# Joint pass with a ring of forty gathered rows, W1 loaded behind the routing loop, and a reordered combining stage

## The reference, cut to what matters

```python
xn = layernorm(x)
x = x + gat(xn, edges, W1, att_src1, att_dst1, b1, W2, att_src2, att_dst2, b2) \
      + mix(xn, w_qkv, w_proj, b_proj, proj_mat)
x = x + moe(layernorm(x), Wr, br, W1, b1, W2, b2, ln_g, ln_b)

def gat(x, edges, ...):       # two layers; self loops are added
    h = elu(gat_layer(x, ..., 4 heads of 512, concatenated))
    return gat_layer(h, ..., 1 head of 768)
def gat_layer(x, src, dst, W, a_src, a_dst, bias):
    h = x @ W
    e = leaky_relu((h * a_src).sum(-1)[src] + (h * a_dst).sum(-1)[dst], 0.2)
    ex = exp(e - segment_max(e, dst)[dst])
    alpha = ex / (segment_sum(ex, dst)[dst] + 1e-16)
    return segment_sum(h[src] * alpha, dst) + bias
def mix(x, ...):              # linear attention, 12 heads of 64, 256 random features
    q, k, v = x @ w_qkv.T
    q1, k1 = features(q), features(k)      # exp(dash - diag - max) + 1e-4
    return (q1 @ (k1.T @ v) / (q1 @ k1.sum(0))) @ w_proj.T + b_proj
def moe(x, ...):              # 8 experts, 768 -> 192 -> 768, the best two of each token
    out = sum over the two of weight * (gelu(x @ W1[e] + b1[e]) @ W2[e] + b2[e])
    return layernorm(out) * ln_g + ln_b
```

## Time and profile before

| | us |
|---|---|
| median of 3 runs (lowest, highest) | 4027.84 (4027.04, 4029.59) |
| the profiled execution, its time | 4029.73 |
| the profiled execution, its span in the trace | 4027.9 |
| TensorE busy in the span | 3300.9 (82%) |
| VectorE busy | 1924.8 (48%) |
| GpSimd busy | 1510.0 (37%) |
| ScalarE busy | 1126.3 (28%) |

### The profile page before, as it was taken

The page is one execution under the profiler, slowest core; times in us unless marked ns, Lnnn a source line. Parts: engine busy times, 40 slices in busy tenths (PEclk is TensorE's granted clock), DMA queues, the critical chain, the costliest instruction groups (busy, mean ns, idle before and its releaser), DMA issues. The chain is left out here.

```text
span 4027.9 us, 62736 instructions
## 1 busy us (share of the span) xinstructions
PE 3300.9 (82%) x21812; PEld 2631.4 (65%) x21813; DVE 1924.8 (48%) x4387; ACT 1126.3 (28%) x2419; POOL 1510.0 (37%) x1514
## 2 busy tenths in 40 slices
PE   7966889889889879999799967887888878569940
PEld 7964666666666658899799955555555545459940
DVE  4844555555555554444322214444444444543347
ACT  2332333333333333333322212222222221313321
POOL 1334656565556400000000025555555552223346
PEclk9988999999999989999899977888898889569975
DMA  6656776776777465444666647777777774837667
GB/s 196 217 174 194 217 224 210 219 224 208 217 225 216 146 185 151 131 133 123 181 99 86 87 135 227 240 246 233 240 238 248 233 235 133 271 112 242 239 220 256
DMA packets 276409, 786.75 MB, mean 195 GB/s; under 512 B 81807, under 2 KB 94818, under 8 KB 272903
## 3 DMA queue, kind: packets, MB, share of 16 engines
q0 software_dynamic: 97216, 416.71, 33.9%
q1 hardware_dynamic: 178886, 366.15, 30.8%
HBM read 676.48 MB, written 167.42 MB: 210 GB/s over the span
## 5 line engine op out<-in xcount | busy, mean ns | idle before, releaser
L937 POOL DMA_INDIRECT k_rows<-tab,k_pick x576 | 583.8, 1014 | 429.3 <-PE k_num L1392 231.3
L2182 POOL DMA_INDIRECT m_rows<-tab,a_e x500 | 498.4, 997 | 449.9 <-PE m_out L2501 249.8
L1392 PE MATMUL k_num<-k_rows,k_wt 128*32 128x385 f32 (+1 forms) x3200 | 346.9, 496 | 71.3 <-issue 51.3
L1392 PEld LDWEIGHTS k_num<-k_rows,k_wt 128*32 128x32 f32 x3200 | 109.7, 110 | 243.0 <-issue 209.1
L142 PE MATMUL g_prod<-g_w_hi,g_h_h 128*128 128x384 f32 x768 | 258.7, 337 | 11.0 <-DVE g_h_l L1802 11.0
L143 PE MATMUL g_prod<-g_w_lo,g_h_h 128*128 128x384 f32 x768 | 258.2, 336 | 0.0
L144 PE MATMUL g_prod<-g_w_hi,g_h_l 128*128 128x384 f32 x768 | 258.1, 336 | 0.0
L1654 PE MATMUL f_prod<-f_a_h,f_w_hi 128*128 128x512 f32 (+1 forms) x672 | 253.8, 378 | 1.8 <-DVE f_w_lo L1597 1.7
L1655 PE MATMUL f_prod<-f_a_l,f_w_hi 128*128 128x512 f32 (+1 forms) x672 | 246.4, 367 | 0.0
L1656 PE MATMUL f_prod<-f_a_h,f_w_lo 128*128 128x512 f32 (+1 forms) x672 | 246.4, 367 | 0.0
L2481 PE MATMUL m_pj<-a_w,m_at 128*128 128x384 f32 x600 | 220.1, 520 | 18.1 <-DVE m_x L2292 17.8
(11 more groups left out here) (367 smaller groups left out, 7596.2 us busy)
## 6 DMA issues: line engine op xcount, KB each, us to landing
agg<-k_outb SPq DMA_DIRECT2D x100, 384.0 KB
f_a_in<-agg SPq DMA_DIRECT2D x100, 384.0 KB, 7.3
g_h<-h SPq DMA_DIRECT2D x25, 1024.0 KB, 12.2
ys<-e_y SPq DMA_DIRECT2D x56, 384.0 KB
h<-f_e SPq DMA_DIRECT2D x16, 1024.0 KB, 5.2
tab<-q_xn SPq DMA_DIRECT2D x25, 388.5 KB, 5.8
tab<-g_row SPq DMA_DIRECT2D x25, 385.5 KB, 4.5
m_own<-tab SPq DMA_DIRECT2D x25, 385.5 KB, 7.4
```

The lines of the kernel that those rows point to most:

```text
L937: pool.indirect_dma_start(rows[:, place(u, n), :], None, dram["tab1"], at, bounds_check=bound, oob_is_err=False).then_inc(rows_in[i], 16)
L1392: mm = pe.matmul(num[i][o, 0:n], wt[u % 2][:, v, o], rows[:, place(u, 2 * (half + v) + g), a:a + n], start=(v == 0), stop=(v == 1), tile_p ...
L2182: pool.indirect_dma_start(rows[:, place(h, c) + k, :], None, tab, bass.IndirectOffsetOnAxis(ap=e[h % 4][:, 0, k * SLOTS + c:k * SLOTS + c ...
```

## The change

In the joint pass the ring has 40 places. Room for it comes from x in three buffers instead of four, and from single buffers for `qt_h`, `att` and `own`; of `own` the two last columns, which the logits need, have a small double buffer of their own (`own_al`). The waits follow: `qt_high` for the products that read `qt_h`, `divide` for the turns that read `att`, `load_own` for the sums of the tile before. GpSimd adds the bias to x behind the gathers of a stage instead of before them. In SP's order `own` is last and the store stands before x. In the routing stage the six loads of W1 stand behind the loop. Six tiles of x for the combining stage are loaded at the end of the experts' stage, into buffers of a pool around both; the combining stage has six buffers for x and three for y, and VectorE adds the second expert of tile t+1 before it finishes tile t.

```diff
@@ mix_out
-    RING = 36
-    XR = 4
+    RING = 40
+    XR = 3
-        qt_h = s.sb2("qt_h", [P, KC, P], F32R)
+        qt_h = s.sb("qt_h", [P, KC, P], F32R)
-        att, at = s.sb2("att", [P, D]), s.sb("at", [P, KC, P])
+        att, at = s.sb("att", [P, D]), s.sb("at", [P, KC, P])
-            ald, own = s.sb2("ald", [P, P]), s.sb2("own", [P, TROW2])
+            ald, own, own_al = s.sb2("ald", [P, P]), s.sb("own", [P, D + 1]), s.sb2("own_al", [P, 2])
@@ mix_out, sync
-                def load_own(h):
+                def load_ends(h):
                     if h >= 2:
                         sp.wait_ge(acc_done, 2 * (h - 1))
                     sp.dma_start(ald[h % 2][:, :], ...).then_inc(ald_in[h % 2], 16)
-                    sp.dma_start(own[h % 2][:, :], tab[h * P:(h + 1) * P, :]).then_inc(own_in[h % 2], 16)
+                    sp.dma_start(own_al[h % 2][:, :], tab[h * P:(h + 1) * P, D + 1:D + 3]).then_inc(own_al_in[h % 2], 16)
+
+                def load_own(h):
+                    if h:
+                        sp.wait_ge(acc_done, 2 * h)
+                    sp.dma_start(own[:, :], tab[h * P:(h + 1) * P, 0:D + 1]).then_inc(own_in, 16)
...
                     if t + 2 < NT:
                         load_q(t + 2)
+                    if merged and 1 <= t < NT:
+                        load_ends(t)
+                    if t >= 2:
+                        store(t - 2)
                     if t + 1 < NT:
                         load_x(t + 1)
-                    if merged and 1 <= t < NT:
+                    if merged and t < NT:
                         load_own(t)
-                    if t >= 2:
-                        store(t - 2)
@@ mix_out, gpsimd
                 for t in range(NT):
+                    if merged and t >= 1:
+                        gathers(t)
                     pool.wait_ge(x_in[t % XR], 16 * (t // XR + 1))
                     pool.tensor_tensor(x[t % XR][:, :], x[t % XR][:, :], bias[:, :], ALU.add).then_inc(xb_done, 1)
-                    if merged and t >= 1:
-                        gathers(t)
@@ mix_out, scalar
                     act.wait_ge(q_in[t % 2], 16 * (t // 2 + 1))
+                    if t:
+                        act.wait_ge(dash_full, 6 * t)
...
                 qt_high(0)
-                qt_high(1)
                 for g in range(6):
                     exps(0, g)
+                qt_high(1)
@@ mix_out, vector
-                    if t >= 2 and i == 0:
-                        dve.wait_ge(atr_full, 2 * t - 2)
-                    if merged and t == 1 and i == 0:
-                        dve.wait_ge(bias_done, 1)
+                    if t and i < 2:
+                        dve.wait_ge(atr_full, 2 * t - 1 + i)
...
+                    if h == 0:
+                        dve.wait_ge(bias_done, 1)
+                    dve.wait_ge(own_in, 16 * (h + 1))
                     dve.wait_ge(slot_done, SLOTS * (h + 1))
...
                 qt_low(0)
-                qt_low(1)
                 for g in range(6):
                     maxima(0, g)
+                qt_low(1)
@@ phase_route, sync (behind the loop over t instead of in tiles 8 to 13)
-                if 8 <= t < 8 + KC:
-                    k = t - 8
-                    sp.dma_start(moe["w1"][:, k, :], io["eW1"][k * P:(k + 1) * P, :]).then_inc(w_in, 16)
+            for k in range(KC):
+                sp.dma_start(moe["w1"][:, k, :], io["eW1"][k * P:(k + 1) * P, :]).then_inc(w_in, 16)
@@ phase_experts, sync
                 sp.dma_start(dram["ys"][j * P:(j + 1) * P, :], y[j % YR][:, :]).then_inc(y_out[j % YR], 16)
+                t = j - (ETILES - REST)
+                if t >= 0:
+                    sp.wait_ge(xs_out[t % SR], 16 * (t // SR + 1))
+                    sp.dma_start(moe["rest"][t][:, :], dram["xs"][t * P:(t + 1) * P, :]).then_inc(moe["rest_in"][t], 16)
@@ phase_combine
+    XR = REST
+    x, x_in = moe["rest"], moe["rest_in"]
-        y = s.sb2("y", [P, D])
+        y = [s.sb(f"y{b}", [P, D]) for b in range(3)]
...
             for t in range(NT):
-                if t + 2 < NT:
-                    load_x(t + 2)
+                if t >= 2 and t + XR - 2 < NT:
+                    load_x(t + XR - 2)
                 store(t)
...
+            both(0)
+            for t in range(NT):
+                b = t % 3
+                dve.wait_ge(y_done, t + 1)
+                if t:
+                    dve.wait_ge(gain_done, t)
+                layernorm_stats(dve, y[b], st, mv, stats_done, stats_seen, mean_done, t)
                 if t == 0:
                     dve.wait_ge(c_in, 16)
                 dve.wait_ge(mean_done, t + 1)
                 dve.scalar_tensor_tensor(out=y[b][:, :], in0=y[b][:, :], scalar=mv[:, 0:1], in1=gain[:, :], op0=ALU.subtract,
                                          op1=ALU.mult).then_inc(gain_done, 1)
+                if t + 1 < NT:
+                    both(t + 1)
+                result(t)
@@ phase_ffn
-        phase_experts(nc, io, dram, keep, moe)
-        phase_combine(nc, io, dram, keep, moe, out)
+        with Pool(nc, "z") as z:
+            moe["rest"], moe["rest_in"] = [z.sb(f"rest{b}", [P, D]) for b in range(REST)], [z.sem(f"rest_in{b}") for b in range(REST)]
+            phase_experts(nc, io, dram, keep, moe)
+            phase_combine(nc, io, dram, keep, moe, out)
```

More of the change, by code:

```diff
@@ L2187, in _ @@
                     pool.wait_ge(bias_in, 32)
-                    pool.tensor_tensor(bias[:, :], bias[:, :], att[1][:, :], ALU.add).then_inc(bias_done, 1)
+                    pool.tensor_tensor(bias[:, :], bias[:, :], acc[:, 0:D], ALU.add).then_inc(bias_done, 1)
                     pool.wait_ge(bias_done, 1)
@@ L2433, in dashes @@
                         pe.wait_ge(exp_done, 12 * t + 2 * g)
[L2434 removed]
+                    dash_pair(pe, dash, qt_h, qt_l[t % 2], g, pj_h, pj_l, dash_full)
                 def turns(t, g):
@@ L3117, in _, with both, result @@
                 act.wait_ge(g_in[0][t % R], 16 * (t // R + 1))
-                if t >= 2:
-                    act.wait_ge(sum_done, t - 1)
-                act.activation(y[t % 2][:, :], g[0][t % R][:, :], ACT.Copy, scale=moe["gate"][:, 0, t:t + 1]).then_inc(part_done, 1)
+                if t >= 3:
+                    act.wait_ge(sum_done, t - 2)
+                act.activation(y[t % 3][:, :], g[0][t % R][:, :], ACT.Copy, scale=moe["gate"][:, 0, t:t + 1]).then_inc(part_done, 1)
         @blk.vector
         def _(dve):
-            for t in range(NT):
-                b = t % 2
+            def both(t):
+                b = t % 3
                 dve.wait_ge(part_done, t + 1)
                 dve.wait_ge(g_in[1][t % R], 16 * (t // R + 1))
+                dve.scalar_tensor_tensor(out=y[b][:, :], in0=g[1][t % R][:, :], scalar=moe["gate"][:, 1, t:t + 1], in1=y[b][:, :],
+                                         op0=ALU.mult, op1=ALU.add).then_inc(y_done, 1)
+            def result(t):
+                b = t % 3
+                dve.wait_ge(gain_done, t + 1)
+                dve.wait_ge(rstd_done, t + 1)
+                dve.wait_ge(x_in[t % XR], 16 * (t // XR + 1))
+                dve.scalar_tensor_tensor(out=x[t % XR][:, :], in0=y[b][:, :], scalar=rstd[:, 0:1], in1=x[t % XR][:, :], op0=ALU.mult,
+                                         op1=ALU.add).then_inc(sum_done, 1)
+            both(0)
+            for t in range(NT):
+                b = t % 3
+                dve.wait_ge(y_done, t + 1)
+                if t:
+                    dve.wait_ge(gain_done, t)
+                layernorm_stats(dve, y[b], st, mv, stats_done, stats_seen, mean_done, t)
                 if t == 0:
                     dve.wait_ge(c_in, 16)
-                dve.scalar_tensor_tensor(out=y[b][:, :], in0=g[1][t % R][:, :], scalar=moe["gate"][:, 1, t:t + 1], in1=y[b][:, :],
-                                         op0=ALU.mult, op1=ALU.add).then_inc(y_done, 1)
-                dve.wait_ge(y_done, t + 1)
-                layernorm_stats(dve, y[b], st, mv, stats_done, stats_seen, mean_done, t)
                 dve.wait_ge(mean_done, t + 1)
@@ L3136, in _ @@
                                          op1=ALU.mult).then_inc(gain_done, 1)
-                dve.wait_ge(gain_done, t + 1)
-                dve.wait_ge(rstd_done, t + 1)
-                dve.wait_ge(x_in[t % R], 16 * (t // R + 1))
-                dve.scalar_tensor_tensor(out=x[t % R][:, :], in0=y[b][:, :], scalar=rstd[:, 0:1], in1=x[t % R][:, :], op0=ALU.mult,
-                                         op1=ALU.add).then_inc(sum_done, 1)
+                if t + 1 < NT:
+                    both(t + 1)
+                result(t)
 def phase_ffn(nc, io, dram, keep, out):
```

39 lines of the change are left out of this document (18 added, 21 removed).

## The result

The changed kernel took 4051.85 us (median) where the kernel before took 4028.53 beside it on the same chip: a ratio of 1.0053, 95% interval 1.0032 to 1.0074. It is slower by 21 us; 4004 was forecast. Its single times spread from 4023 to 4082, against 4013 to 4040 before, without the executions that fell in a slower state (three and one). The profiled execution, at 4033, is among its faster ones, so the profile shows only a part of the loss.

The account below looks back on a forecast made before the run. TensorE is busy 82% of the span, but no one stage rules the rest, so each touched place was read by its own waits. From 4027.8, -11 - 5 - 3 + 0.5 - 7 + 2 = -23.5 gives 4004 us; range 3968 to 4030.

Parts of the forecast that it names:

- part 4 to 6: Joint pass: longer ring, addition to x behind the gathers, new SP queue; together -0.3 us a stage, 23 stages, -7 us.
- part 6: Joint pass, SP's queue with three x buffers and single own: 0 taken; load of x in the burst +28 at worst.
- Stage 22: Joint-pass stage without edge loads: logits start 15.5 us after first gather, not 20.3; next first gather unchanged, so 0.
- Part 4: Joint pass, ring of 40: gathers lead by four more, nobody waits for rows; 0 us.
- Part 5: Joint pass, addition to x leaves the gather burst: 1.7 us a stage shorter burst, -37 us if late signals follow.
- its condition: Joint pass: room from slot 2 must come in time for the third gather group; otherwise the shorter burst gives nothing.
- The rival: Joint pass slower: moved addition holds VectorE at L2292, TensorE waits; 0.57 to 1 us a stage, up to +23; chance 0.23.
- Part 7: Joint pass, single att and qt_h: tile 1's query halves come later, delaying TensorE once; +2 us.
- Part 1: Routing: six W1 loads leave the saturated stretch, seven tiles return to 3.47 us each; -11 us.
- Part 2: Combining: both(t+1) before result(t) partly covers VectorE's wait for GpSimd's rstd; -5 us, bounds 0 and -11.
- The bound of 11 us: Combining: with DMA share at 0.91, only 0.09 of each 5.25 us tile over 24 tiles can come back.
- Part 3: Start of combining: six x tiles loaded in the experts' tail, -3 us; barrier from the outer pool's semaphores, +0.5.

Follow-up runs that it names:

- part 5 alone: Kernel before with new routing and combining, single att and qt_h, and the addition to x ahead of the burst: 3542.1 us against 3560.1, 0.9950.
- the first experiment: Changed kernel with the joint pass of the kernel before; W1 behind the routing loop and new combining stay: 3973.3 us, 0.9940 to the kernel before.
- The ladder: Kernel before (3994 us) with new routing and combining; then single att and qt_h; new SP queue; ring of 40, addition inside burst: 3973.3, 3968.7, 3991.8, 3999.8 us.

## Why the prediction was wrong

**The failed step** is part 4 to 6 with "for 4 to 6 together I take -0.3 us a stage". In sessions like the trace's it is +1 us a stage for part 6 (23 us in one session, 20 in another), and some 1 us more, read in part across sessions, for the ring and the addition's place. In part 6 I had priced the load of x in the burst (up to +28) and taken 0 for the edge loads and own, because "all these are used a half stage later". The load of x does nothing in a 40-us stage (0.9932 against 0.9926), and the rest of the part costs. My argument looked only for who waits for the data. What was at stake was when TensorE gets its instructions and signals through; I wrote that these come late while gathers burst, and then let the order in SP's queue have no part in it. Stage 22, which I used to dismiss it, was a hint that was not followed up: without edge loads the late result came 4.8 us earlier in the stage, so the loads did touch the thing. I had written "what was won early was lost late" and made it 0. Where it was lost can be read in that stage of the trace before: its gathers go out as four, the addition and twelve, and then

```profile
3322.74 6.40 PE L2481 MATMUL m_pj<-a_w,m_at 128*128 128x384 f32 x12
```

a projection at the lower clock, where the stage of the earlier trace rows has 4.04 us. The changed queue makes every stage one without edge loads in the burst. The sum has no term for the clock.

**Part 4, ring of 40: 0.** Its lead is worth nothing, as said, and no wait for the landing of rows appeared. It isn't free, though: with the addition inside the burst the ring of 40 took 8 us more than the ring of 36.

**Part 5, the burst.** In 40-us stages its condition failed, by the late signal and not by slot 2's sums: no first group of twelve appeared. What I had not followed further is that with the ring of 40 slot 4's group changes sides and makes the second group twelve. So twelve gathers in a row, priced at -1.7 us a stage, stand in the profile's 44-us stages and not in its 39-us ones. Where stages take 29 us, part 5 alone costs some 6 us (0.9950 against 0.9933), where VectorE is held; a stage is longer by 0.5 us. The rival's size (0.57 to 1 us) was about right, its victim was another.

**Part 7, +2**: 5 us less by the medians, inside the intervals: nothing that can be told.

**Part 1, -11**: right, -10.5. The tile behind W1's old place is 3.4 us, and W1 is issued behind the loop, under the tail:

```profile
3513.58 0.68 DVE L2692 TENSOR_SCALAR r_xn<-r_x,r_mv,r_rstd 128x768 f32<-128x768 f32 x1
...
3516.95 0.68 DVE L2692 TENSOR_SCALAR r_xn<-r_x,r_mv,r_rstd 128x768 f32<-128x768 f32 x1
...
3556.12 3.06 SPq L2626 DMA_DIRECT2D w_w<-in_eW  x6
```

From the last tile to TensorE's first work on an expert it is 3.3 us more, so perhaps not all of the cover was free.

**Part 2, -5**: the mechanism right, the term mis-sized, -17.2. Two tiles of the combining stage, in order of time:

```profile
3941.12 1.04 DVE L3162 SCALAR_TENSOR_TENSOR o_y<-o_y,o_mv,o_gain 128x768 f32<-128x768 f32 x1
3941.17 0.18 POOL L194 TENSOR_TENSOR o_vps<-o_mv,keep_ln_eps 128x1 f32<-128x1 f32 x1
3941.43 1.16 POOL L196 TENSOR_TENSOR o_rstd<-o_vps,keep_minus_half 128x1 f32<-128x1 f32 x1
3942.08 1.00 DVE L3141 SCALAR_TENSOR_TENSOR o_y<-o_g,w_gate,o_y 128x768 f32<-128x768 f32 x1
...
3943.01 1.01 DVE L3149 SCALAR_TENSOR_TENSOR z_rest<-o_y,o_rstd,z_rest 128x768 f32<-128x768 f32 x1
...
3945.34 1.02 DVE L3162 SCALAR_TENSOR_TENSOR o_y<-o_y,o_mv,o_gain 128x768 f32<-128x768 f32 x1
3945.39 1.01 POOL L194 TENSOR_TENSOR o_vps<-o_mv,keep_ln_eps 128x1 f32<-128x1 f32 x1 [0.17 <-DVE o_mv L188]
3946.48 0.56 POOL L196 TENSOR_TENSOR o_rstd<-o_vps,keep_minus_half 128x1 f32<-128x1 f32 x1
```

GpSimd's pair is held by gain once, either in the addition or in the power, and ends 0.4 to 0.7 us behind gain. It is not held again by `both`, which stands ahead of `result` and covers it: no wait for rstd is left, 24 x 0.78 = 19 us, where I had taken 0.28 a tile; some 5 us of new waits for gathers stand against it. The bound of 11 us from the DMA share fell as well: the share rose to 0.97, and the rate from 299 to 338 GB/s with it, so a share of 0.91 at 299 was no ceiling.

**Part 3, -3 and +0.5**: -2.4 and up to +1.6. As said.

**Sum.** With the measured terms in sessions of the trace's kind: -10.5 - 2.4 - 17.2 + 1.6 + 4.5 for the ends and what lies between is -24.0, in line with the 21 to 24 of the first experiment; the change as a whole is +21 by its ratio, so the joint pass gave back some 45. The ladder has 23 for part 6, about 8 for the ring, 17, read across sessions, for the addition's place, and -5 for part 7, 43 in all. Where the kernel before takes 3560 us the same change is a gain of 16 us (0.9956), 13 us of joint pass being lost there (703.7 against 690.7), where the hold of VectorE stands.

**What beats both kernels.** Everything but parts 4 to 6: 0.9926 in one kind of session, 0.9933 in the other. No other version ran in both kinds and was ahead in both.

## What to carry to other kernels

A small DMA that nobody waits for may still set when other engines make headway: before a load is moved at price 0, look at what stands late beside its old place and its new one, not only at who reads it. Where one stage of a trace happens to lack the load, read that stage to its end, the granted clock and the length of TensorE's groups included. Against GpSimd count every VectorE operation with two SBUF operands, its own neighbours and those that a longer or shorter stage would bring beside it. And a share of busy DMA engines is no ceiling unless the rate in GB/s beside it has been seen to be the highest.

## What the runs showed of the hardware

- The same kernel has two speeds, by session: 3551 to 3562 us or 3994 to 4038, all of it in the two passes over the edges (joint pass 690.7 or 910.6 us); the gathers of the experts' stage take 264 us in either. In the slower kind TensorE's instructions come 0.70 us apart late in a burst, and others go on up to 8.5 us after the product that they wait for has ended, at 229 to 246 GB/s; in the faster kind neither happens at 325 GB/s. The same change has other signs in the two (0.9956 against 1.0053).
- In the slower kind a projection of twelve matmuls takes 4.04 us at the upper clock and up to 7.2 at the lower one, to which it falls where TensorE had little to do late in a burst.
- A VectorE operation of two SBUF operands, 1.02 us, took 1.80 beside a GpSimd addition of 1.82, ending 0.83 us behind it; in the slower sessions' changed kernel it never met the addition, and all 25 took 1.02.
- Where the addition on GpSimd waits for its load, 1.7 us a stage, in the kernel with the ring of 40, a stage of 29.3 us is longer by 0.8.
